# A two-layer transformer on one core: the written-out issue orders of all engines replaced, and the causal mask given a step of its own

## The reference

```
# per image (256 x 128)
q, k, v = x @ Wq, x @ Wkv                      # 16 heads of 64
x1 = LN(x + softmax(q k^T * scale) v @ Wo + bo)
# feed-forward with a router: 8 clusters of 8 tiles, argmax of spline gates
h    = gelu(x1 @ cw1 + cb1);  comp = tanh(h @ cw2 + cb2)
tile = argmax(cluster gates), argmax(tile gates inside)
x2   = LN(x1 + mag(comp, spline[tile]) * directions[tile] * 0.1)
# mixer: 16 heads of 8, a linear attention and a window of 65 keys
lin  = linear attention of elu(.)+1
loc  = softmax over offsets -32..32 of (q_s . k_{s+off} * scale + rel_bias[off]), times v
g    = gate from [x2, lin, loc] (wg1, wg2)
x3   = LN(x2 + (g * lin + (1-g) * loc) @ wo + bo)
# layer 2, per image (256 tokens)
h  = LN(x3) * ln_g + ln_b;  q, k, v = h @ Wq, h @ Wk, h @ Wv          # 16 heads of 64
q, k = q/|q| * q_scale, k/|k| * k_scale
o  = softmax(where(causal, 10 q k^T, -1e9)) v @ Wo
h  = LN(o);  gate = softmax(h @ gate_w + gate_b)                      # 8 experts, all computed
moe = sum_e gate_e * (gelu(h @ w1_e + b1_e) @ w2_e + b2_e)
y  = LN(x3 + LN(moe))
```

## Time and profile before

| what | value |
|---|---|
| three runs | 2449.78, 2451.48, 2452.81 us; median 2451.48 |
| the profiled execution | 2448.45 us; span 2446.7, so 1.75 lie around the span |
| mean granted clock of PE | 0.961 |
| PE busy | 2219.9 us (91%), 16096 instructions |
| DVE, ACT, POOL busy | 1570.6 (64%), 1366.2 (56%), 848.0 us (35%) |
| mixed parts | 293 us each; first part 218, last part 174 |

### The profile page before, as it was taken

One profiled execution on the slowest core, in us unless ns is written; L12 is line 12 of the kernel. 1 busy time (PEld: TensorE's weight loads), 2 busy tenths in 40 slices (PEclk: granted clock), 3 DMA queues, 4 the chain that ended last, 5 costly groups with the idle time before them and its releaser, 6 DMA issues.

```text
span 2446.7 us, 43966 instructions
## 1 busy us (share of the span) xinstructions
PE 2219.9 (91%) x16096; PEld 1544.8 (63%) x16096; DVE 1570.6 (64%) x4247; ACT 1366.2 (56%) x3798; POOL 848.0 (35%) x1010
## 2 busy tenths in 40 slices
PE   7758998999989999999999999899998989999797
PEld 5545656756668566675666765676666756667465
DVE  4566676576656766667665767657676676666742
ACT  4436573755647655476555756465563764546442
POOL 2313461045510544106431256113561054510630
PEclk9878999999999999999999999999999999998899
DMA  4000000000010000110001000000001000010001
GB/s 145 27 1 1 1 10 27 18 31 1 10 35 10 31 10 1 44 31 2 10 1 44 32 1 10 18 27 31 1 10 33 13 31 1 1 35 10 31 1 48
DMA packets 24561, 50.43 MB, mean 21 GB/s; under 512 B 3285, under 2 KB 3869, under 8 KB 23965
## 3 DMA queue, kind: packets, MB, share of 16 engines
q1 hardware_dynamic: 24348, 47.62, 6.0%
HBM read 45.52 MB, written 2.10 MB: 19 GB/s over the span
## 4 chain that ended last, share of the span: by engine, by line
PE 71%; DVE 14%; POOL 6%; issue 5%; ACT 4%; DVEq 0%; ACTq 0%; POOLq 0%
PE ps L1439 9%; PE ps L1460 9%; PE ps L865 5%; PE ps L638 5%; PE ps L833 4%; PE ps L1396 4%; PE ps L655 4%; PE ps L1379 3%; PE ps L1472 3%; PE ps L593 3%; PE ps L1336 3%; PE ps L1347 3%; PE ps L747 3%; PE ps L764 2%; PE ps L800 2%
## 5 line engine op out<-in xcount | busy, mean ns | idle before, releaser
L1005 POOL TENSOR_TENSOR rstd<-ve,half_neg 128x4 f32<-128x4 f32 (+1 forms) x56 | 66.9, 1194 | 1016.1 <-DVE ve L986 1016.1
L1460 PEld LDWEIGHTS ps<-wbuf,QK 128*128 128x128 f32 x2048 | 265.4, 191 | 108.9 <-issue 101.6
L1259 POOL TENSOR_TENSOR E<-E,ri 128x512 f32<-128x512 f32 x240 | 248.3, 1041 | 192.8 <-DVE ri L1058 192.7
L1563 ACT ACTIVATE QK<-ps,cols 128x512 f32<-128x512 f32 x256 | 172.9, 686 | 219.0 <-PE ps L1439 218.6
L888 ACT ACTIVATE E<-ps,nm 128x256 f32<-128x256 f32 x480 | 224.7, 481 | 107.7 <-DVE nm L1051 106.8
L1439 PE MATMUL ps<-h2T,wbuf 128*128 128x512 f32 x512 | 277.9, 632 | 0.2
L1460 PE MATMUL ps<-wbuf,QK 128*128 128x128 f32 x2048 | 269.0, 275 | 0.2
L1689 POOL TENSOR_TENSOR work<-work,ri 128x128 f32<-128x128 f32 x480 | 231.4, 508 | 103.5 <-DVE ri L1612 103.3
L1682 POOL TENSOR_TENSOR rn<-ss,half_neg 128x8 f32<-128x8 f32 x120 | 195.7, 1638 | 168.7 <-DVE ss L1588 167.8
L1523 ACT ACTIVATE work<-ps,nm 128x128 f32<-128x128 f32 x480 | 198.9, 427 | 73.8 <-DVE nm L1603 72.6
L1051 DVE TENSOR_REDUCE nm<-ps 128x2 f32<-128x512 f32 x256 | 168.8, 684 | 65.2 <-PE ps L638 64.1
(11 more groups left out here) (279 smaller groups left out, 4537.3 us busy)
## 6 DMA issues: line engine op xcount, KB each, us to landing
wbuf<-in_w SPq DMA_DIRECT2D x128, 256.0 KB, 3.2
xT<-in_xT SPq DMA_DIRECT2D x8, 256.0 KB, 2.7
xr<-in_xr SPq DMA_DIRECT2D x8, 256.0 KB, 3.0
bias_t<-in_bias_t SPq DMA_DIRECT2D x1, 2048.0 KB
out_y<-xn SPq DMA_DIRECT2D x8, 256.0 KB, 2.1
wqkv<-in_wqkv SPq DMA_DIRECT2D x1, 1536.0 KB
wo<-in_wo SPq DMA_DIRECT2D x2, 512.0 KB, 8.8
rows<-in_rows SPq DMA_DIRECT2D x1, 531.0 KB, 7.1
```

The source lines that it names most:

```text
L1259: nc.gpsimd.tensor_tensor(L.E[:, g % 4, :, :], L.E[:, g % 4, :, :], L.ri[:, g, :].unsqueeze(2).broadcast_to((P, NT, S)), ALU.mult)\
L1460: last = nc.tensor.matmul(bank2[2 + x % 2][:, t * P:(t + 1) * P], hid[:, x % 2, c, t * P:(t + 1) * P], w2[:, x % WB, c, :], start=(c == 0) ...
```

## The change

There are two edits. The first replaces the digits of the strings in ORDER, for all engines and kinds of part (and renames the kind "second" to "last"). The second puts a `yield` between the mask matmuls and the score matmuls of the second attention, so each of the 20 mask units of a part on PE becomes two steps; the strings of PE grow by 20 digits where that attention runs. No instruction of arithmetic is added or taken away on any engine; on ACT the number of table loads is the same, and some stand elsewhere.

```
     ("first", "tensor"):
-        "010111101111110010111100000010000111111010011000011001001001100110011011010010101001110010011110"
-        "00001100102200000200000000000000000000000000000000000000000000000202200222222",
+        "101010000000101100100001111010011110000111000101100101100101101101011010101101100110001101100001"
+        "11110011010000000000020000000000000000000000200000000000200000000202200222222",
...
-KINDS = ["first", "both", "both", "second"]
+KINDS = ["first", "both", "both", "last"]
...
@@ -1373,6 +1374,8 @@
                         nc.tensor.matmul(tri(L.bank[i][:, 0:384], 3)[:, 0::2, :], ident_bf[:, :],
                                          causal[:, :].unsqueeze(1).broadcast_to((P, 2, P)),
                                          start=True, stop=False, skip_group_check=True)
+                yield
+                if u < HP:
                     for t, o in ((0, slice(0, P)), (1, slice(P, 3 * P))):
                         for i in range(2):
                             r = DH * i
```

More of the change, by code:

```diff
@@ L73 @@
-        "000000111110000001001101100001111111011101001000000000000000000000000000100000000000000000100010"
-        "000010001100000100000101011101010000000000111101011111011011000000000010",
+        "001000011111110011111101100011011011111111111111111000011111101110100001011101000000111101001111"
+        "010011101100001110011000000011111010000011110011111011111101111111110111111101111101111111111111"
+        "111001111110111000001010111010000101101100000111110000001111010000010111100000111101000110011100"
@@ L79 @@
-        "000000001001000000000022000002000202200222222",
+        "000011111111101100110101111011110110110101111100001101100011101101110100111110011101000111011101"
+        "000111100111101111110110101111111111000101101101101111011011000011111100011110000111010110101101"
+        "001110000110111010110111010011010001111100000111111001101001011111111111110111111111011110111001"
+        "11000110000000000000000000000100100000000020000022000202200222222",
     ("both", "scalar"):
-        "110000111111011010011111011000111111110000111100001111000011111111000011110000011110001111111111"
@@ L82 @@
[L82 to L83 removed]
+        "110010011111110010011111011000111111110000111100001111000011111111000011110000011110001111111111"
+        "110111111110011101111101111111100000111100001111000011110000111100001111000011110000111100000111"
+        "110001110101110111111011111111111111011010111001100110000000000000000000000000000000002222022222"
@@ L84 @@
         "222",
     ("both", "gpsimd"):
-        "000111010111100001010111010101011001111111111111101001100101010101010101010110011010000000110",
+        "000111001111100001101010101110100110111111111111100100111010100011011001011010101010000000110",
     ("both", "sync"):
-        "1110111111",
-    ("second", "vector"):
-        "000000000000001000111111101001110110110101110011111011110111111110000111111000001110000001000101"
-        "111000010111100001011101000101111000100111100001011100100011111000100111100000111000110010000000"
+        "1111110111",
@@ L92 @@
+    ("last", "vector"):
+        "000000000000010000111111101001111100110111101001111011111111011110011000111100001110000000001101"
+        "111010000111100010011110000011101110000111010000111110000001111100010111100000111000110010000000"
         "00000000000000000000000000000000000",
-    ("second", "tensor"):
-        "000100000011001011111001100110111010111110110011001001111000001110001111001010010110100101011001"
-        "00011110010110100111001001111000001100100000000000000000000000000000000000000",
@@ L96 @@
-    ("second", "scalar"):
-        "000000001001011110011000111111001111111111000000001111000011110000111100001111000011110000111100"
-        "001111000011111000001101000000000000000000000000000000000000",
-    ("second", "gpsimd"):
-        "000011101101110011001100110010101010101110001100000",
+    ("last", "tensor"):
+        "001000000010011011111001100111100101011111110011001001111100000011110010011110000111010001011100"
+        "010111010100011011001001011101000111100100011111000000110010000000000000000000000000000000000000"
+        "0",
@@ L101 @@
+    ("last", "scalar"):
+        "000000000010111110011000111001111111111111000000001111000011110000111100001111000011110000111100"
+        "001111000011111000001110000000000000000000000000000000000000",
+    ("last", "gpsimd"):
+        "000011101101110011010100110010110001101010110100000",
 }
-KINDS = ["first", "both", "both", "second"]
+KINDS = ["first", "both", "both", "last"]
 def merged(order, *programs):
```

22 lines of the change are left out of this document (8 added, 14 removed).

## The result

The changed kernel takes 2415.23 us (median of four runs, 2414.5 to 2416.53), the kernel before 2450.63 (four runs, 2449.18 to 2452.81): a ratio of 0.9855, 95% interval 0.9838 to 0.9872, 35.4 us less. The forecast was 15 less, with a range down to 2418. The sign was right; the size was more than twice the forecast, and the time lies outside the range.

A forecast was written before the change was run, and what follows sets the result against it. TensorE was taken as the bound, busy 2219.9 of 2446.7 us, so only its idle time and half-clock stretches could yield. Terms -7.7 - 5 - 3.5 + 3.9 - 3 = -15.3 took 2451.5 to 2436 us, range 2418 to 2455.

The forecast's parts named there:

- Boundary: End of mixed parts: scores issued before transposes fill PE's wait for x; 1.1 us sooner, -7.7 over seven (-8.3 to 0).
- The clock at the boundary: Half-clock dips at six of seven part boundaries cost 9.7 us; half assumed gone, -5 (-9.7 to 0).
- Image b: Second attention's mask: 1/sum ahead of the maxima lets POOL and PE start sooner; -0.5 a part, -3.5 (-6 to +3.5).
- Start of the experts: Last values of attention two go ahead of wo0, so x1 comes some 0.5 later; +0.56 a part, +3.9 (-4 to +9).
- Table loads: ACT: exponential ec moved behind two GELUs with two loads, 2.77 us fitting in 3.13 idle; cost 0, uncovered 2.8 a part.
- The rest of a mixed part: Router chain, window scores and expert products reordered, same work; 0, between -1 and +2 us a part.
- First part: Three projections moved into the window stage, where waits and a half-clock dip stand; -3 us (-6 to +3).
- (a): Rival, more gain: all six boundary dips go, POOL's gain counts whole, experts' start costs nothing; -29.4, 2422 us; chance 0.20.
- (d): Rival, slower: the half-clock stretch at the experts' start grows, 3.4 us a part, +24, 2460 us; chance 0.16.
- (b): Rival, no change: the boundary's gain is lost at the experts' start, dips stay; 2451 us; chance 0.15.
- (c): Rival: ACT's table loads don't fit their cover, 2.4 us a part, +17, 2453 us; chance 0.03.

The follow-up runs named there:

- warm2: Changed kernel plus transposes nobody reads in many TensorE waits, in all parts, including the first part's two long waits: 2398.47 us for 2452.59, ratio 0.9780.
- warm3: Like warm2 on the changed kernel, one or two fewer transposes per place in mixed parts, only 45 in the last part: 2398.26 us for 2450.62, ratio 0.9790.
- bnd: Kernel before, with only TensorE's first scores issued ahead of the transposes of xn3 in the seven mixed parts: 2432.74 us for 2446.41, ratio 0.9943.
- imgb: Kernel before, with only the changed orders of all engines for image b's attention in the mixed parts: 2454.82 us for 2446.41, ratio 1.0033.
- wo: Kernel before, mixed parts: only last values of attention two moved ahead of wo0's products, copy QK ahead of the residual sum: 2448.25 us for 2446.41, ratio 1.0017.
- shim: Kernel with changed boundary, image b and end of attentions, plus 8 unread transposes ahead of image a's wo2 products: 2427.99 us, against 2429.88 without them.
- shift: Changed kernel plus 24 unread transposes, 2.6 us, once at the start of the first mixed part: 2418.58 us for 2450.62, ratio 0.9871.

## Why the prediction was wrong

*Boundary, -7.7.* Right: 1.06 a part in the table's kernels, 7.4.

*The clock at the boundary, -5 (-9.7 to 0).* All six stretches went, in the trace of every kernel with the new boundary; only warm2 and warm3 have one at the boundary of the last part. I had taken half. The mechanism was right, the size at the bound. What the step did not see is that the stretch at the experts' start does not stay: it was 6.8 throughout in bnd's trace, and 6.8, 17.1, 10.2 by turns in the changed kernel's.

*Image b, -3.5.* The parts of the term are in the trace: the POOL waits of 1.6 went, a new one of 1.15 came, 0.47 less, at -0.5 forecast. Alone it is worth nothing: imgb has another wait of 0.53 before wo0. The term was right only together with the end of the attentions.

*Start of the experts, +3.9.* This step failed in its sign for the changed kernel. I gave the chain 0.3 back for the copy QK's own 0.42 and left out that the copy waited 0.46 for L1396 before it ran, which stands in its row. With both gone wo0's end to x1 is 4.3 for 5.1, in wo and in the changed kernel alike. In wo, the experiment that has this change alone, x1 still came 0.6 later, close to the 0.5 forecast. That was luck: 0.8 was given back instead of 0.3, and wo0 started 1.4 later instead of 0.8. With image b's orders L1399 is fed in time, and the two places give -1.1 a part at the gating, not +0.06: 7.7 us less, where the two terms make 0.4 more. The wait before x1's transposes came as said, 0.71 for the 0.9.

*Table loads, 0.* Right by little. The load takes 1.28 and the exponential follows at once, no drain. But the cover of 3.13 is nearly used up: in the changed kernel L1442 waits for the GELU in three parts, 0.7 in all:

```profile
PE ps L1374 <- ACT work L1526: 9.5, 14, 1.2
...
PE ps L639 <- ACT ETw L1321: 4.1, 6, 0.7
...
PE ps L1442 <- ACT QK L1566: 0.7, 3, 0.3
```

The first of these lines is the new wait of image b, the second the 0.69 before the first scores. In warm2, where PE runs at full clock, PE waits 1.1 a part for that GELU.

*The rest of a mixed part, 0 (-1 to +2 a part).* This step failed, and most of all: the q and k stage of image a gave 0.8 and the late stage 0.9 a part, 1.7 together and 12 us in seven, outside the bounds of the term. In the last mixed part the late stage gave 4.4. The term had been put at nothing because the work is the same, and the order of the q and k stage does not stand in it at all.

*First part, -3.* It gave 1.1 between the two traces, and the kernel with that part alone was 0.17% (0.07 to 0.27) faster, 4 us. The first part's length differs from trace to trace: 218.0 to 221.2, in the middle 219.8, in the eight kernels with its old orders, and 216.1 to 218.2, in the middle 216.9, in the seven with the new ones and no fillers there. That makes 2.9, as forecast. The stretch at 195.7 did go in the changed kernel, and another grew from 3.4 to 13.7; in four of the other six with the new orders one of 3.4 or 6.8 is left near there. Busy time of two stretches:

```profile
195.70:205.90 10.20, 9.78 (x132) 8.29 (x131) 3.87 (x8) 6.33 (x16) 0.00 (x0) 1.00 0.01 2
...
158.00:172.00 14.00, 10.25 (x50) 9.11 (x51) 7.04 (x12) 3.38 (x10) 1.98 (x1) 0.52 0.00 0
```

*The rivals.* (a), more, was the nearest: it had all boundary stretches gone and 2422, without the two stages. (d) half came: the stretches at the experts' start did grow, from 65 to 75 us in all. They were 17.1 in two parts of seven, each 3.7 longer than the parts with 6.8, and shorter than before in two. (b) and (c) did not come.

*The sum.* For the stages of the mixed parts it had -7.7 - 3.5 + 3.9 = -7.3, where the table gives -24. The pieces are 7.4 (boundary), 5.6 (image a), 7.7 (image b and the end of the attentions) and 6.3 (late stage), 27 together, of which 3 are lost again between the gating and the gate products. So 12 us come from the rest that was put at nothing, and 8 from the two terms that held only together: the orders of DVE, ACT and PE win jointly, where I had priced single moves. For the clock in the mixed parts it had -5 and 8.7 came. There it took a price for each place, where a stretch depends on when its stage comes, as shim and shift show; why a given order of part lengths comes out, and so what the sum would be for another kernel, stays open.

## What to carry to other kernels

In a kernel that repeats one stage many times with PE near its limit, look at the granted clock part by part before pricing waits: in one execution gains below a microsecond a part can be hidden or swelled by where the half-clock stretches then fall. Judge a change first by parts with equal stretches, then by ratios over several runs, and look whether the profiled run is a typical one. Read the wait in a moved row's own brackets as part of the chain it leaves. Orders of several engines fit together: cut or undo them on all engines at one place, and test pairs together before calling a half useless. And where PE must wait, work that nobody reads can be cheaper than a clock that halves: here it won 16 to 18 us.

## What the runs showed of the hardware

- The same sequence gave stretches of 6.8, 10.2 and 17.1 us at half the granted clock in different parts of the changed kernel, with no wait of PE above 1.6 us in such a part. After one delay of 2.6 us at the start, the fifth to seventh mixed part had other stretches, the second to fourth the same.
- With 0.86 us more PE work in each of seven parts, a kernel was no slower beyond the noise (2427.99 and 2429.88).
- Filling waits of 0.3 to 1.6 us with transposes took the granted clock from 0.97 to 0.99 up to 1.00 in six of the seven mixed parts (warm2). With the first part's two long waits filled too, its longest stretch fell from 48 us to 10.
- A table load took 1.28 us on ACT, with the next activation 0.01 behind it.
